# First edge loop of a graph kernel: the stages of a group of tiles spread over eight steps instead of six

## The reference

```python
h = x @ W1 + b1
h_i, h_j = h[dst], h[src]
e = concatenate([h_i, h_j - h_i], axis=-1)
m = relu(e @ W2 + b2)
m = relu(m @ W3 + b3)
out = relu(segment_max(m, dst))
x = layernorm(x + out)
```

## Time and profile before

| what | us |
| --- | --- |
| median of 3 runs | 5114.23 (5113.04 to 5115.49) |
| the profiled execution | 5080.73 |
| its span, first to last instruction | 5079.0 |
| TensorE busy over the span | 3026.1 (60%) |
| GpSimd busy | 3101.8 (61%) |
| VectorE busy | 2397.1 (47%) |
| ScalarE busy | 1573.5 (31%) |
| mean granted share of TensorE's clock | 0.734 |

### The profile page before, as it was taken

How to read it: one execution, slowest core, us unless ns; L and a number is a source line. 1 busy time by engine, 2 the same in 40 slices (tenths; PEclk the granted TensorE clock), 3 DMA queues, 4 the chain that set the end, 5 groups by cost and what they waited for, 6 DMA issues and landing times.

```text
span 5079.0 us, 59955 instructions
## 1 busy us (share of the span) xinstructions
PE 3026.1 (60%) x16577; PEld 2418.2 (48%) x16577; DVE 2397.1 (47%) x7909; ACT 1573.5 (31%) x2400; POOL 3101.8 (61%) x3256
## 2 busy tenths in 40 slices
PE   3677777777777777777743444444444444444346
PEld 2566566666665655566613333433333434333343
DVE  3355454545554554454613444444444434444466
ACT  1343444444444444444522212222122212212213
POOL 5666666666666666666255666666666666666630
PEclk6788888888888899888855565555656556556667
DMA  6444444444444444444222222222222222222221
GB/s 153 134 131 141 132 129 138 136 130 137 136 132 124 147 133 124 146 131 128 80 77 58 68 75 68 75 68 69 74 69 71 72 69 74 69 71 73 68 70 52
DMA packets 416487, 512.07 MB, mean 101 GB/s; under 512 B 102420, under 2 KB 335310, under 8 KB 416153
## 3 DMA queue, kind: packets, MB, share of 16 engines
q1 hardware_dynamic: 301833, 288.42, 17.8%
q0 software_dynamic: 105056, 217.07, 17.4%
q10 hardware_dynamic: 9266, 2.75, 0.3%
HBM read 492.20 MB, written 15.68 MB: 100 GB/s over the span
## 4 chain that ended last, share of the span: by engine, by line
another core or an unknown queue 33%; PE 31%; issue 17%; ACT 9%; DVE 8%; DVEq 1%; DMA 1%; ACTq 1%
PE bank L784 7%; PE bank L791 7%; PE bank L808 6%; DVE Z L1254 3%; PE bank L783 3%; PE bank L799 3%; ACT Z L630 2%; PE bank L905 1%; DVE Z L1243 1%; ACT Z L566 1%; ACT Z L637 1%; ACT Z L561 1%; ACT Z L573 1%; ACT Z L580 1%
## 5 line engine op out<-in xcount | busy, mean ns | idle before, releaser
L480 POOL DMA_INDIRECT G<-q_tab,srcT x1612 | 1535.9, 953 | 889.8 <-issue 420.8
L480 POOL DMA_INDIRECT G<-x_tab,srcT x832 | 792.2, 952 | 472.2 <-issue 235.4
L1097 DVE TENSOR_TENSOR accT<-accT,bank 128x128 f32 x1612 | 454.9, 282 | 1138.3 <-remote 767.4
L480 POOL DMA_INDIRECT X<-x_tab,srcT x780 | 744.1, 954 | 372.9 <-issue 219.3
L784 PE MATMUL bank<-Z 128*128 128x128 f32 x3224 | 675.5, 304 | 135.5 <-issue 133.6
L905 PE MATMUL bank<-Z,G 128*128 128x128 f32 x1664 | 380.6, 394 | 569.2 <-DVE Z L1243 244.1
L905 PE MATMUL bank<-Z,X 128*128 128x128 f32 x1560 | 369.1, 405 | 531.7 <-DVE Z L1243 274.7
L1254 DVE SCALAR_TENSOR_TENSOR Z<-Z,evr,bank 128x128 f32 x1612 | 552.6, 343 | 210.7 <-issue 129.0
L784 PEld LDWEIGHTS bank<-Z 128*128 128x128 f32 x3224 | 570.0, 217 | 156.9 <-issue 155.8
L1243 DVE TENSOR_SCALAR Z<-iota,relT,evr 128x128 f32<-128x128 f32 x1612 | 571.5, 365 | 113.1 <-ACT evr L660 86.5
L905 PEld LDWEIGHTS bank<-Z,G 128*128 128x128 f32 x1664 | 324.0, 287 | 613.5 <-issue 328.4
(11 more groups left out here) (200 smaller groups left out, 2961.2 us busy)
## 6 DMA issues: line engine op xcount, KB each, us to landing
Z<-p_tab SPq DMA_DIRECT2D x1612, 64.0 KB
Z<-meta SPq DMA_DIRECT2D x62, 896.0 KB
Z<-meta SPq DMA_DIRECT2D x61, 832.0 KB
Z<-meta SPq DMA_DIRECT2D x62, 768.0 KB
G<-q_tab,srcT POOLq DMA_INDIRECT x1612
G<-x_tab,srcT POOLq DMA_INDIRECT x832
X<-x_tab,srcT POOLq DMA_INDIRECT x780
x_tab<-X SPq DMA_DIRECT2D x13, 264.0 KB, 2.1
```

The lines of the kernel that those rows point to most:

```text
L480: return pool.indirect_dma_start(to, None, of, bass.IndirectOffsetOnAxis(ap=srcT[:, t:t + 1], axis=0))
L1097: v.tensor_tensor(win, win, bank[6 + k % 2][:, j * 128:(j + 1) * 128], ALU.add).then_inc(acc_ok, 1)
```

## The change

Every stage behind `pre` is moved to a later step, the end picks and the scan too; on VectorE the scan goes to the end of the step, on TensorE the pick to its beginning. Waits are added where the new order no longer implies that a buffer is free, and so that they can be written for all groups.

```diff
             def relu(k, g):
-                if k == 3:
-                    act.wait_ge(v_mm, 1)
+                if 3 <= k < 5:
+                    act.wait_ge(v_mm, k - 2)
                 act.wait_ge(x_mm, k + 1)
...
             def evac(k, g):
-                if k + 3 >= K0:
+                if k + 4 >= K0:
                     act.wait_ge(o_mm, k - 2)
...
-            groups([(0, distance), (0, one_hot), (1, relu), (4, evac)])
+            groups([(0, distance), (0, one_hot), (2, relu), (6, evac)])
...
             def pre(k, g):
                 i = k // GROUPS
+                after(pe, relu_ok, k - 1)
                 pe.wait_ge(landed[g], i * 64 + 64)
...
             def tr_s(k, g):
-                if k + 3 >= K0:
-                    pe.wait_ge(st_ok, k - 1)
+                after(pe, st_ok, k - 1)
                 pe.wait_ge(scan_ok, k + 1)
...
             def pick(k, g):
-                if k + 5 >= K0:
-                    pe.wait_ge(st_ok, k + 1)
+                after(pe, acc_ok, GT * (k - 1))
+                pe.wait_ge(st_ok, k + 1)
                 pe.wait_ge(eoh_ok, k + 1)
...
-            groups([(0, pre), (1, mm3), (3, tr_s), (5, pick)])
+            groups([(7, pick), (0, pre), (2, mm3), (4, tr_s)])
...
             def scan(k, g):
+                if 3 <= k < 5:
+                    dve.wait_ge(s_tr, k - 2)
                 after(dve, scan_ok, k)
...
-            groups([(0, x_product), (6, add_up(0)), (2, scan), (6, add_up(1)), (4, ends(0)), (6, add_up(2)), (4, ends(1)), (6, add_up(3)), (4, ends(2, 3))])
+            groups([(0, x_product), (8, add_up(0)), (5, ends(0)), (8, add_up(1)), (5, ends(1)), (8, add_up(2)), (5, ends(2, 3)), (8, add_up(3)), (3, scan)])
```

## The result

The kernel after takes 5120.1 us (median of 20 runs, 5117.6 to 5122.3) where the kernel before takes 5114.1 in the same sessions (20 runs, 5110.1 to 5122.2): ratio 1.0012, 95% interval 1.0006 to 1.0017. A later session gave 5082.4 against 5075.8, ratio 1.0018 (1.0009 to 1.0028). So the change costs about 6 us and gains nothing. The forecast of 5062 was wrong; the second rival, "nothing moves" at 5119, came nearest.

What follows compares the result with a forecast made beforehand. It took GpSimd's gathers, 5.03 us a group, plus pauses ended by TensorE's late marks as the bound, 5.91 us together. 5080.7 - 57 (longer runs) + 5 (drain) = 5029 profiled, 5062 on the median; 8-in-10 range 4960 to 5170.

Steps and rivals of the forecast that it cites:

- nothing moves: Rival for the first layer's loop: marks come through only at pauses, so only the drain counts; 5119 us, chance 0.20.
- GpSimd's 5.03 us a group: First layer's loop: 4 gathers of 0.95 us with 0.31 us between them, GpSimd's time for a group without pauses.
- The reserves: How late a mark may be before TensorE stops: relu 2.9 to 5.1 us, copy 2.4 to 5.9, pick 3.2 to 4.2.
- idle within groups that grows by what the waits lose: Sign of a wrong forecast: TensorE's idle inside groups grows by as much as its waits shrink.
- I expect runs of two and three groups, 10 gathers on the mean: GpSimd's gathers between pauses lengthen from 6.5 to 10; 0.15 us less a group, 57 us over 380 groups.
- price of 1.80 us for a pause: GpSimd's pause after 10 gathers, interpolated between 1.44 us at 6.5 and 1.89 at 10.9; gives 5.75 us a group.
- The mean pause of 1.44 us: GpSimd's 166 pauses in 271 groups, 1.75 us each, 1.44 above the usual gap between gathers.
- The drain: Two more steps at the loop's end, at no more than 3.52 us each; taken as 5 us together.
- The broadcast at 0: SyncE's transfer of lists starts later, with 13.7 us left for a transfer of 13.7 us; costed at 0.
- All waits of TensorE go: Rival: reserves above the 4.6 us delay remove TensorE's waits; 220 us less, 4899, or 4788 through the clock; chance 0.12.
- its sign, as many pauses as before: Sign of the rival "nothing moves": GpSimd pauses as often as today, 166 times in 271 groups.
- "Slower" by the pick ahead of `pre`: Rival: `pre` behind the pick releases gathers 0.89 us later; 5159 us, or 5326 if at all 166 pauses; chance 0.25.

Runs made afterwards that it cites:

- the usual sessions: All measurement rounds but one; there the unchanged kernel before took 5114.1 us, or 5075.8 in a later session.
- forced runs: GpSimd's gathers wait only ahead of every second group, so 8 run together; 5078.7 us in the kernel before, 5084.4 in the kernel after, against 5075.9 for before unchanged.
- the forced kernel: The kernel before, with GpSimd's gathers waiting only ahead of every second group: 5078.7 us, ratio 1.0005 to before.
- the last kernel: The kernel after, with GpSimd's gathers waiting only ahead of every second group: 5084.4 us, ratio 1.0017 to before.
- the quick session: One round of measurements on one chip in which the unchanged kernel before took 4312.5 us; the same chip gave 5075.8 in a later one.

## Why the prediction was wrong

**What bounds the kernel.** Right: marks of TensorE come late while gathers follow one another, and with GpSimd's pauses. Runs without gathers, with plain DMAs and with landings awaited all bear it out. Incomplete: I took GpSimd's 5.03 us a group as its price and the pauses as something that the placement of the others decides. In the usual sessions the price of a gather is about 1.48 us, 5.9 us a group, with the pauses in it.

**The reserves.** Each was sized against the delay seen, 4.6 us. The relu's went to 5.1, and TensorE's idle before W3 fell as said. But the delay isn't a fixed length: most marks wait for the next quiet of GpSimd, and GpSimd goes quiet when its ring of 13 groups is full. As the consumers moved back, relu's delay went from 4.4 to 5.9 us. And what TensorE no longer waited it stood still in the middle of groups: the line "idle within groups that grows by what the waits lose", among the signs of a wrong forecast, is what came, 237 to 269 us, and with forced runs it was 304 of 376 us.

**The step that failed** is "I expect runs of two and three groups, 10 gathers on the mean", with its price of 1.80 us for a pause. The runs became shorter, 1071 / 203 = 5.3; no run shows why. And between 4 and 8 gathers their length hardly matters: the run of eight of the forced kernel is 7 x 1.25 + 3.04 = 11.8 us, 5.9 a group, a run of four 3 x 1.25 + 2.2 = 5.95. The mean pause of 1.44 us that I interpolated from was a mix of 0.95 after 4 gathers (51 times) and 1.73 after 8 (110 times), which is 0.24 and 0.22 us a gather: nearly in proportion, so that only a small fixed part is there to save. At 10 gathers the same rows, with 2.25 after the second layer's runs of 12, give about 2.0 and not 1.80. The view of GpSimd's timeline, sorted by the length of the run ahead of each pause, would have shown it in the trace of before. The second layer's runs of 16 come to (15 x 1.25 + 4.1) / 16 = 1.43 us a gather, 0.05 less than the first layer's; whether runs that long would bring the first layer the same 0.2 us a group wasn't tried.

**The drain** was taken at 5 us and is 1.8 to 1.9.

**The broadcast at 0**: right. Without it and without the windows a group of the kernel after takes 5.926 us, with them 5.982 and 5.928 in its two traces.

**The rivals.** "All waits of TensorE go" nearly had its condition in the last kernel, and the time didn't follow: waits weren't what the pace hung on. "Nothing moves" named a reason that holds in the main, marks at pauses, and gave 5119. That it lies within 1 us is in part luck: its drain was too large by some 3 us, the period grew instead, and its sign, as many pauses as before, isn't quite there (203 in 268 groups). "Slower" by the pick ahead of `pre`: neither more pauses ended by L785 directly (23 instead of 32) nor idle ahead of the pick's first matmul (8 us in 1600) is there. What the remaining 4 us or so are made of wasn't settled; the profile shows only that a pause after a run of the same length is somewhat longer, 0.07 us with forced runs, 0.01 to 0.04 between the traces of 5080.7 and 5075.9 us.

## What stays open

What in the chip takes 1.48 us for an indirect gather that GpSimd issues in 1.25 and whose bytes have moved after 2.2, and holds marks beside it, isn't shown by any run. Nor is why one session didn't have it, on the same chip. The Trainium skill (DMA: Bandwidth & Descriptors, section Latency and other measured facts) offers, as a guess at why two of the DMA engines are slow, that the descriptor rings of GpSimd's DMAs lie in SBUF, behind ports that also serve those two engines. No run here shows those ports, and half the rows left the pace as it was.

## What to carry to other kernels

When several engines resume at the same moment after idling, don't size reserves against the delay you see: ask what ends it, and whether that event moves with your change. Sort the pauses of the engine that stands out by the work ahead of them; if their length is in proportion to it, they belong to that engine's price, and a reordering of its consumers has little to recover. And force the lever by hand first, as with the runs of eight here: a two-line edit showed that it was worth nothing up to there.

## What the runs showed of the hardware

- Indirect gathers of 128 rows back to back on GpSimd cost about 1.48 us each in the usual sessions (1071 to 1084 in 1600 us in nine traces, whose normal step was 1.20 to 1.38 us), 1.46 in the second layer, 1.45 over a first run of 56, and 1.25 in the quick session. The kernel before took 4313 us in one session and 5076 in another on the same chip, with the same instructions.
- The bytes of such a gather have moved 2.2 us after its start (median), at any place in a run and in either kind of session.
- From about the fourth of such gathers in a run, few of TensorE's marks come through until GpSimd has been quiet for 1 us after 4 gathers and 2 us after 8 (beside the fifth to seventh gather some 440 fall due and 120 arrive in before, some 515 and under 40 where the gathers wait for the relu). After a full stop they are prompt beside the next two or three gathers. A mark of GpSimd to itself was held as well (2.02 us ahead of the memset behind the 41st gather).
- While marks are held, TensorE itself slows: matmuls of one stage that wait for nothing start mostly 0.7 or 1.3 us apart, and nearly all of that idle time falls beside the sixth to eighth gather of a run (235 of 237 us in before). In the kernels without gathers, with plain DMAs, with landings awaited and in those of the quick session no such gap over 0.1 us is found.
- A plain DMA of as many bytes in consecutive rows on GpSimd's queue (0.54 us) leaves the marks prompt, and so does a kernel without gathers.
- A memset of one column behind a gather (0.12 us) lies wholly in the 0.30 us between two gathers; one of 128x176 bf16 (0.26 us) lengthens the step to 1.38 us.
